# Decoder kernel in two lanes: the written-out order of the lanes' work on each engine is replaced by another one

## The reference

```
x = ln(x + L0_attn(x))          # relative positions, attention over 4 positions of time
x = ln(x + L0_xattn(x, ctx))    # 16 heads over 77 context tokens, boolean mask
x = ln(x + L0_ffn(x))           # one expert chosen for a whole sequence
x = ln(x + L1_attn(x))          # "bump": out_i = sum_j max(0, 1 - |zq_i - zk_j| / b_h) * v_j / 512
x = ln(x + L1_xattn(x, ctx))    # 16 heads over 77 context tokens, integer mask
x = ln(x + L1_ffn(x))           # 2 x (causal self-attention, 16 heads of 8, then a mixture of 8 experts)
```

## Time and profile before

| what | value |
|---|---|
| time, median of 3 runs | 1313.42 us (1313.33 to 1319.65) |
| the profiled execution, its own time | 1321.68 us |
| its span | 1319.8 us |
| TensorE clock granted, mean over the span | 0.834 of full speed |
| PE busy | 1065.3 us, 81% of the span |
| PE weight loads busy | 618.7 us, 47% |
| DVE busy | 785.8 us, 60% |
| ACT busy | 642.5 us, 49% |
| POOL busy | 380.5 us, 29% |

### The profile page before, as it was taken

One profiled execution on the slowest core, in us unless ns is written; L12 is line 12 of the kernel. 1 busy time (PEld: TensorE's weight loads), 2 busy tenths in 40 slices (PEclk: granted clock), 3 DMA queues, 4 the chain that ended last, 5 costly groups with the idle time before them and its releaser, 6 DMA issues. The chain is left out here.

```text
span 1319.8 us, 20146 instructions
## 1 busy us (share of the span) xinstructions
PE 1065.3 (81%) x7223; PEld 618.7 (47%) x7286; DVE 785.8 (60%) x2021; ACT 642.5 (49%) x1252; POOL 380.5 (29%) x771
## 2 busy tenths in 40 slices
PE   7858666888879879579997866789879969949986
PEld 6755322243434469544465431233244448924454
DVE  3664676666596640497436487775778542279453
ACT  2114349853327536317643539863315736515851
POOL 3032120332124531514403111313213442342520
PEclk8778759677589969879998969885668979979998
DMA  8022000202330035550013100102042024452020
GB/s 296 21 62 65 11 1 1 57 14 53 99 102 3 10 113 193 160 130 4 19 48 107 36 11 0 39 19 57 29 121 54 2 95 161 134 169 48 3 65 17
DMA packets 70722, 86.67 MB, mean 66 GB/s; under 512 B 18614, under 2 KB 58854, under 8 KB 70119
## 3 DMA queue, kind: packets, MB, share of 16 engines
q1 hardware_dynamic: 67710, 80.70, 21.4%
q0 software_dynamic: 2048, 4.20, 1.1%
q10 hardware_dynamic: 864, 0.48, 0.1%
HBM read 55.90 MB, written 28.86 MB: 64 GB/s over the span
## 5 line engine op out<-in xcount | busy, mean ns | idle before, releaser
L1571 DVE TENSOR_REDUCE sb_rmax<-banks 128x1 f32<-128x384 f32 (+3 forms) x352 | 206.6, 636 | 67.3 <-PE banks L1419 66.1
L1500 ACT ACTIVATE sb_arena<-banks 128x512 f32<-128x512 f32 x320 | 176.8, 597 | 106.0 <-PE banks L1430 100.2
L1320 ACT ACTIVATE sb_arena<-banks,sb_zk 128x512 f32<-128x512 f32 x256 | 153.7, 746 | 15.8 <-PE banks L1270 10.7
L1417 PE MATMUL banks<-sb_arena,sb_qs 128*128 128x256 bf16 (+3 forms) x489 | 124.6, 327 | 37.4 <-DMA sb_arena<-k_scratch 19.4
L1526 POOL TENSOR_SCALAR_AFFINE_SELECT sb_arena<-sb_arena 128x256 f32<-128x256 f32 x256 | 99.2, 409 | 183.1 <-ACT sb_arena L1500 183.0
L480 POOL TENSOR_SCALAR sb_var<-sb_mv 128x4 f32<-128x4 f32 x40 | 13.1, 328 | 376.6 <-DVE sb_mv L465 376.6
L1054 ACT ACTIVATE sb_arena<-banks 77x512 f32<-77x512 f32 x128 | 73.4, 589 | 91.6 <-PE banks L967 73.4
L1430 PE MATMUL banks<-sb_qs,sb_arena 128*128 128x512 bf16 (+3 forms) x495 | 104.0, 302 | 13.1 <-DVE sb_rmax L1571 3.2
L1366 DVE TENSOR_SCALAR sb_arena<-sb_arena,sb_bw 128x2048 f32<-128x2048 f32 x64 | 90.1, 1420 | 28.3 <-ACT sb_arena L1320 28.1
L1419 PE MATMUL banks<-sb_trib,sb_identb 128*128 128x128 bf16 (+2 forms) x352 | 93.0, 264 | 7.0 <-DVE sb_rmax L1571 5.1
L1417 PEld LDWEIGHTS banks<-sb_arena,sb_qs 128*128 128x128 bf16 x512 | 48.3, 105 | 106.2 <-DVE sb_rmax L1571 47.2
(11 more groups left out here) (352 smaller groups left out, 2200.4 us busy)
## 6 DMA issues: line engine op xcount, KB each, us to landing
sb_arena<-in_chosen SPq DMA_DIRECT2D x28, 514.0 KB, 4.5
sb_qs<-q_scratch SPq DMA_DIRECT2D x32, 288.0 KB, 4.8
q_scratch<-sb_region SPq DMA_DIRECT2D x16, 384.0 KB, 2.6
sb_arena<-k_scratch SPq DMA_DIRECT2D x16, 288.0 KB, 6.8
sb_qs<-in_chosen SPq DMA_DIRECT2D x8, 514.0 KB, 5.2
sb_w<-in_w SPq DMA_DIRECT2D x2, 2048.0 KB
q_scratch<-sb_region SPq DMA_DIRECT2D x16, 256.0 KB, 2.2
done<-sb_arena SPq DMA_DIRECT2D x28, 128.0 KB, 4.1
```

What stands on the lines that cost most here:

```text
L1320: i = nc.scalar.activation(L.dist[h % 3][:, kb, :], (b2_, b3)[h % 2], ACT.Abs, bias=L.zk[:, kb, h:h + 1])
L1417: nc.tensor.matmul(o[:, i * kl:(i + 1) * kl], L.qs[:, h // 2, t * 128:kl], L.ks[:, key_of(h), 0:kl], start=(i == 0), stop=False)
L1500: nc.scalar.activation(L.probs[:, u % SLOTS, :], bank_of(SELF_ORDER, ring, ("key", u)), ACT.Exp)\
L1571: nc.vector.tensor_reduce(L.rmax[:, t, g * GROUP + h0:g * GROUP + h0 + nh], bank_of(SELF_ORDER, ring, ("max", step))[:, 0:nh * kl] .rearra ...
```

## The change

The five strings of `ORDER` are replaced. They have the same lengths and the same numbers of turns of each lane; nothing else in the file differs, so that each lane executes the same instructions in the same order as before, and only their interleaving on each engine is another. The table was computed by a planner that is not part of the file; the change is described as made by a model whose TensorE clock follows the rows and columns that are in use. One line of each of two engines:

```diff
     "SP":
-    "285ae923e00ff811df2e06c2bf80fe566006f743f801ff8077cb81b0afe03f95998",
+    "2855d923e00ff901fe560d859f80fe566006f743f801ff807f5581b0afe03f55998",
     "PE":
-    "803f81f3270000070378ff187e00e080c01c000c6effffffefffef15410014200157ef7f80c0c2788368028000007df9fb00"
...
+    "803783cf270000004de3fc787e00e0018038001c6effffffefffef1490200520012fbdfe3300939883580c0001ff7ff391c1"
...
```

More of the change, by code:

```diff
@@ L185 @@
+    "00902000007000f007e00078dfbfffff7ffbfffffbb144408a04004bf77f8c90303e20f8140003effde4e44c220070000273"
+    "bfffffffbff7fffeec04540006aa4a90a32244ca854c1292619c9c494925244700c5effff7dfdfffffeefffd10a0001eaaaa"
+    "fffffc008540005d24a90a32244ca854c1292619c9c494925244700c5effffdfbffffffddfeea0481ffffc",
     "ACT":
-    "c03ce9001ffe00f80884041dffffbe9600500df3003fc6437fe0038001bffae0000ffffffffe0000007f02545525280c17fd"
-    "fdffffff2000f6affe00003ffff8001fc0a55555251528a80c1efff7ffe825fe000c1ffc0000000fbffdfdffd250000df200"
@@ L188 @@
-    "7fc5a437fe000003effeb80003ffffffff8000003f811515494a0305ff7fdfffffc8003dabff80000ffffe0007f029555549"
-    "454a2a0307bffdfffa093fe",
+    "c03cd9001ffe00f804040c1dffffbe9480240de400ffc643ffc07330080dffefdfc0001ffffe0003f8125554aa1629480c1d"
+    "ffdfff7f4003daabfe00003ffff80003f812655252949480c1bffbfdfff20bfe000c1ffc0000000fbffdfdffd24824037900"
+    "3ff191ffe038950006fffbf7f00007ffff800003f80a529529450083bfdfdfffffc8003dabff80000ffffe00000fe0294a54"
+    "a514020effdfdfff9f20ffe",
     "POOL":
-    "81e38d8b600cfe30003fffe0000003ff800e619867000fdfffdbcfff0ff8008001fffffe0001ffc01c333319c30c3000ffef"
@@ L192 @@
[L192 to L193 removed]
+    "81e38b8b600fcf80003fffe0001ffc00730cc670cc30003ffbfffff00ff80160007ffffe0001ffc001cc3199c30c000ffeff"
+    "ffff81ce723e00fcf80003fffe000007ff001cc199870c003f7ffdedffe0ff8008001fffffe000007ff001cc199870c003f7"
+    "fffffff98",
     "DVE":
[L195 to L196 removed]
@@ L197 @@
-    "d104449188264080001fff6f5e5f7fe3ffff0f1a100d5500d5aaaaadaabfffea5d83ff868407901aaa003fed56b55556955f"
-    "ff805fd01fe",
+    "003f00fe1f8b80005be000001ffffffff80299d965407071b17442210a2a92079ff9390003e7ede3dffff8c3f00d55000ffa"
+    "ad555555a95fffe015df8b4086cd55000aaaaab555555d49fffd603fc832780082a000001ff5f5cfffffe063e5a9515072b1"
+    "7442211526a019ff39380007b7b7e3dffff853e20352a006ad56aaab5aabfff99703ff868407900d4a801ab55aaaad6aafff"
+    "e65c3f941fe",
 }
```

11 lines of the change are left out of this document (2 added, 9 removed).

## The result

| | before | changed |
|---|---|---|
| median of the runs compared | 1316.54 us (4 runs, 1313.33 to 1322.10) | 1302.45 us (4 runs, 1298.92 to 1302.75) |
| ratio | | 0.9868, 95% interval 0.9821 to 0.9915 |
| profiled execution, span | 1319.8 us | 1300.9 us |
| granted clock, mean over the span | 0.834 | 0.852 |

The change makes the kernel faster by 1.3%. The quotient of the two medians alone is 0.9893, inside the interval. The time lies in the predicted range and 7 us under the predicted value; it also lies in the range of the clock rival (1299.4, in 1295 to 1304), at its upper end.

What follows compares the result with a forecast made beforehand. PE was taken as the likely bound overall, often at half clock, with ACT the bound in BU. Terms -4 - 2 + 2 + 1 - 1 = -4 us gave a median of 1309.4 us, range 1296 to 1323.

Steps and rivals of the forecast that it cites:

- the clock rival: Second half's X1 to S0's beginning: another mixture of products raises the clock, -10 us more, 1299.4 us; chance 0.26.
- The likeliest case: Whole kernel: the summed terms give -4 us, median 1309.4 us, range 1304 to 1315; chance 0.42.
- the one that gave the clock no term in the sum: X1 and S0's beginning: the sum took no clock change; the second half's S0 move counted +1 us.
- The prediction's sign of being wrong: Stretches whose order hardly changed differing by more than some 3 us, which only the clock could do.
- all else: A, X0 and second half's M0: instructions exchange places on engines not waited for there; 0 us.
- BU, second half: Lane 1's copies move among lane 0's heads, removing 5.1 us of ACT waits; -4 us, bounds -7 and 0.
- BU, first half: Lane 0's v copy goes ahead of lane 1's blending, so its tiles start earlier; -2 us, bounds -4 and 0.
- S0's beginning, first half: Lane 0's transposes and k's projection move later, costing lane 0 4 to 8 us; +2 us, bounds 0 and +10.
- The warning that an idle gap would close the clock at S0's start: By the Trainium skill's rule, the new 4 to 8 us gap would slow the clock, a further loss; not summed.
- M0, first half: Lane 0's M0 chain has 13 instead of 29 of lane 1's L1430 beside it; counted 0 us.
- the slower rival: First half's M0: lane 0's chain loses 14.4 us of cover by lane 1's products, giving 1323.8 us; chance 0.23.
- End of the program: S1 and M1: lane 0 favoured, more of M1 overlaps lane 1's S1; -1 us, bounds -3 and +2.

Runs made afterwards that it cites:

- the two comparisons: Changed kernel measured twice against the kernel before, the second time with no edit and 6 runs: ratios 0.9868 and 0.9812.
- with 128 rows: Old order, X1's product L967 replaced by one of the same columns over all 128 rows, maxima not taken off: 0.9805 against the kernel before.
- With 12 rows: Control in the old order: L967 replaced by identity times part of q over 12 rows, maxima not taken off: 1.0032 against the kernel before.

## Why the prediction was right or wrong

The range held the time, and faster was the most likely of the three signs, but by a hair. The likeliest case, 1309.4 us, was not what happened: the forecast was 4 us less than the profiled execution, the two comparisons give 17 us and 25 us less than before. So it was not this case's mechanism that brought the time into the range, and that is luck as far as the sum goes. The step that failed is the one that gave the clock no term in the sum ("X1's products are all small in both lanes, and shifting a lane by a few units need not alter what PE does there"). What the runs showed in its place: the second half's X1 to S0 alone gives 7 us (0.9947), at a clock of 0.74 instead of 0.56 to 0.65, where the sum had +1. The rival for the clock had the place, the sign and nearly the size: it said -10. The size came from comparing the halves of one execution in the earlier trace rows, and over seven executions the old order's stretch is 3 us shorter than in that one. The prediction's sign of being wrong, stretches of unchanged order that differ by over 3 us, can be given by chance alone: the second half's X1 to S0 took 87.9 and 79.0 us in two executions of one order.

*Stage A (0 predicted, about 3 us measured).* The sum had it under "all else", for engines that are not waited for. In both profiles PE's transposes of X0 come 3 to 4 us earlier (81.51 and 82.53 us against 85.76). Up to lane 0's F0 PE idles 33 us both before and in the kernel with only this part changed, and is busy 111.2 us before and 108.1 there.

*BU, second half (-4 predicted, nothing measured).* The move itself went as said. ACT in the changed kernel, from lane 0's last heads to lane 1's first ones, against the earlier trace rows:

```profile
821.22 7.21 ACT L1320 ACTIVATE sb_arena<-banks,sb_zk 128x512 f32<-128x512 f32 x12
828.05 0.96 ACT L1311 ACTIVATE sb_region<-banks,sb_bw 128x512 f32<-128x512 f32 x1
829.50 2.42 ACT L1320 ACTIVATE sb_arena<-banks,sb_zk 128x512 f32<-128x512 f32 x4 [0.48 <-PE banks L1261]
836.68 7.04 ACT L1320 ACTIVATE sb_arena<-banks,sb_zk 128x512 f32<-128x512 f32 x12 [4.76 <-PE banks L1270]
```

The waits of 5.1 us are gone, and one of 4.76 us stands in their place, three heads on. The fourth head needs the sums of the first, and these stand on PE behind what closes lane 0's BU:

```profile
829.25 3.46 PE L1296 MATMUL banks<-sb_fold,sb_region 128*128 128x32 f32 x16
832.52 0.61 PE L1261 MATMUL banks<-sb_k,sb_selb 96*128 96x512 bf16 x1
832.93 1.76 PE L1296 MATMUL banks<-sb_fold,sb_region 128*128 128x32 f32 x8
834.62 1.94 PE L1270 MATMUL banks<-sb_arena 128*32 128x512 f32 x8
```

The prediction stopped one wait too early: it asked what held lane 1's first head and not what would hold its fourth, though the first half's term was worked out by just that rule. The clock had its part in this too. These PE rows ran at 1.2 GHz (eight L1270 in 1.94 us; 1.06 us before, when 827 to 836 were granted 1.00), and the wait of 3.8 to 4.8 us is in all five profiles that have the new order here.

*BU, first half (-2).* DVE has the v copy at 173.21 ahead of the L1223 at 174.66, and ACT's first tiles begin at 174.86; lane 0's BU began at 162.0 against 167.4 before. From there to the first tiles it is 12.9 us, 16.7 before, so the start gained 3.8 us. At X1's start lane 0 was 6.5 us early, of which 5.4 it had brought along: 1 of the 2 us survived. This pair makes the size look right. Over all profiles lane 0 takes 72.6 to 78.3 us from its BU (L1304) to its X1 (L1034) in the five kernels with the new order there, and 76.7 to 82.9 in the nine with the old one, so the term was rather too small than too large. This half's BU was not tried by itself.

*S0's beginning, first half (+2).* The gap came as described, and k's projection at 340.48:

```profile
340.48 2.01 PE L1407 MATMUL banks<-sb_ft,sb_w 128*128 128x512 f32 x2
...
352.95 0.59 PE L1417 MATMUL banks<-sb_arena,sb_qs 128*128 128x128 bf16 x4 [5.34 <-DMA sb_arena<-k_scratch]
```

But lane 0 lost nothing by it. From its transposes (332.28) to its first scores it took 20.7 us; before, from 337.51, 23.6. What the prediction called late in the queue was late in instructions only: the transposes came 5.2 us earlier than before, since X1 ahead of them ran faster (287 to 327 us granted 0.82, before 0.71), and k's projection stood 8.2 us behind them, before 8.3, where the prediction had put it at 354. Lane 1, which was to gain nothing, finished X1 at 347.6 instead of 361.3. The warning that an idle gap would close the clock at S0's start can be judged by the same stretch: PE idled 5.3 us here and yet was granted 0.62 from 325 to 353, where before it had 0.59 from 327 to 367 without the gap. The Trainium skill (TensorE: Matmul & The Clock Gate, Part 1) tells of activity as how busy PE is; in these runs it was not that alone, since with 128 rows PE was busy a smaller share of the time (78% against 87%) and its clock higher.

*M0, first half (0, and the slower rival).* The rival's mechanism is in the profile. The chain of lane 0's M0 in the changed kernel, and the tiles behind it, against the earlier trace rows:

```profile
438.00:471.00 33.00, 22.05 (x157) 14.68 (x158) 18.16 (x83) 9.88 (x20) 14.79 (x24) 0.73 0.27 91
471.00:503.00 32.00, 29.93 (x256) 28.85 (x254) 7.31 (x28) 21.63 (x65) 7.80 (x8) 0.96 0.53 185
```

PE is idle 11.0 us instead of 6.9, so the cover did shrink, by 4 us and not by the 10 from which the rival was to decide. Behind it PE is busy 29.93 of 32 us instead of 26.41. Lane 1, 12 us ahead at its M0 in this profile, is 3 us ahead at its last stage of the first half. That is where most of the first half's gain went, and why the half gives 0.4%. The kernel with the new order everywhere but in X1 to S0 shows the loss by itself: its lane 1 is 7.6 us early at X1 and 1.4 us late at S1. The rival's direction was right and its price, 14.4 us, too high.

*End of the program (-1).* Within what was measured (0.9969), but by the profiles named there the term was too small rather than right. The last 17.9 us have 6.23 us of PE in them, as the earlier trace rows had 6.13: a chain that this order does not shorten.

## What to carry to other kernels

When a stretch is bound by PE and its granted clock is low, ask how many rows of the array its matmuls use before asking how busy PE is: padding a product of few rows to 128 cost no time on PE here and brought the clock back. Treat a low clock in one trace as partly chance: look at the same stretch in several executions before hanging 10 us on it, since here the second one happened to be the odd one. And when a wait goes, follow the engine on to the next instruction that needs the same partner; here that was three heads further.

## What the runs showed of the hardware that was not expected

The rows of one kind of product in one stage (64 of 7286 matmuls) moved the whole kernel by 2.0%, and with zero weights in the added rows still by 1.1%. With 12 rows PE was granted 0.60 and 0.50 over 85 us while busy 87% of them; with 128 rows 0.82 and 0.83 while busy 78% of 69 us. Runs of one program differed by up to 27 us on one chip, following the clock, while those of the changed order lay within 4 us in each of two sets (4 and 6 runs). In the second half's X1 to S0 the new order's gain is gone once L967 has 128 rows. What in the new order raises the clock elsewhere, in stage A and around the first half's BU above all, stays open.
